# Matmuls of a pairwise interaction in 32x64 instead of 32x128 tiles, two field groups in each diagonal slot, and a reordered start

## What is computed

```python
e = jnp.stack([tbl_0[ids[:, 0]], ..., tbl_39[ids[:, 39]]], axis=1)      # 2048 x 40 x 32
iidx, jidx = jnp.triu_indices(40, k=1)
z = jnp.einsum('bpd,pde,bpe->bp', e[:, iidx, :], bilinear_matrices, e[:, jidx, :])
h = jnp.concatenate([z, dense_ctx], axis=1)                              # 2048 x 796
h = jnp.maximum(h @ W_top1 + b_top1, 0.0)                                # 512
h = jnp.maximum(h @ W_top2 + b_top2, 0.0)                                # 256
y = h @ W_top3
```

## Time and profile before

| what | value |
|---|---|
| median of 3 runs | 701.48 us (701.09 to 701.56) |
| profiled execution, own time | 700.91 us |
| its span in the profile | 699.1 us |
| PE busy | 662.1 us, 95% |
| DVE busy | 550.6 us, 79% |
| POOL busy | 463.0 us, 66% |
| ACT busy | 140.3 us, 20% |

### The profile page before, as it was taken

How to read it: one execution, slowest core, us unless ns; L and a number is a source line. 1 busy time by engine, 2 the same in 40 slices (tenths; PEclk the granted TensorE clock), 3 DMA queues, 4 the chain that set the end, 5 groups by cost and what they waited for, 6 DMA issues and landing times.

```text
span 699.1 us, 25209 instructions
## 1 busy us (share of the span) xinstructions
PE 662.1 (95%) x11496; PEld 413.8 (59%) x11496; DVE 550.6 (79%) x630; ACT 140.3 (20%) x350; POOL 463.0 (66%) x494
## 2 busy tenths in 40 slices
PE   1769989999999999999999999999999999999998
PEld 0645655566666666656655656565665656565656
DVE  5788889887898787878888787888878787678860
ACT  5411202112221202220220112211131112310002
POOL 6777777777777777777777777777777777700000
PEclk9999999999999999999999999999999999999999
DMA  6480102111120100200112000210101100000000
GB/s 201 133 294 16 16 15 51 25 16 15 16 61 16 16 15 16 61 15 16 16 20 57 16 15 16 61 16 15 16 16 16 16 15 16 16 4 2 3 1 1
DMA packets 23500, 23.89 MB, mean 34 GB/s; under 512 B 10917, under 2 KB 20705, under 8 KB 23265
## 3 DMA queue, kind: packets, MB, share of 16 engines
q0 software_dynamic: 15360, 7.90, 7.3%
q1 hardware_dynamic: 7418, 13.80, 5.9%
q10 hardware_dynamic: 616, 0.58, 0.3%
HBM read 22.18 MB, written 0.06 MB: 32 GB/s over the span
## 4 chain that ended last, share of the span: by engine, by line
PE 88%; DVE 6%; ACT 2%; issue 2%; DMA 1%; SPq 0%; ACTq 0%; DVEq 0%
PE Y L531 26%; PE ZL L558 24%; PE ZL L583 16%; PE H L509 8%; PE Y L539 6%; PE H L495 5%; DVE prod L760 4%; DVE one L746 2%; ACT xcols L668 1%; PE Y L592 1%; PE Y L601 1%; DVE prod L766 1%; DMA idx<-ids 1%; PE H L592 0%; DMA tab<-tbl 0%
## 5 line engine op out<-in xcount | busy, mean ns | idle before, releaser
L469 POOL DMA_INDIRECT rows<-tbl,idx x480 | 461.5, 962 | 148.1 <-issue 145.4
L760 DVE TENSOR_TENSOR prod<-Y,xcols 128x1024 f32<-128x1024 f32 x296 | 348.6, 1218 | 72.7 <-PE Y L531 72.4
L531 PE MATMUL Y<-xcols,mats 32*128 32x256 f32 x2880 | 207.7, 401 | 12.1 <-DVE prod L760 5.1
L558 PE MATMUL ZL<-prod,sel 128*32 128x256 f32 x3200 | 217.5, 383 | 0.9 <-ACT z L675 0.2
L531 PEld LDWEIGHTS Y<-xcols,mats 32*128 32x128 f32 x2880 | 132.5, 184 | 91.9 <-issue 74.2
L766 DVE TENSOR_TENSOR prod<-Y,xcols 128x1024 f32<-128x1024 f32 x104 | 122.8, 1219 | 46.0 <-PE Y L531 29.7
L668 ACT ACTIVATE xcols<-H 32x256 f32<-32x256 f32 (+3 forms) x223 | 83.8, 376 | 322.1 <-PE H L495 213.2
L558 PEld LDWEIGHTS ZL<-prod,sel 128*32 128x32 f32 x3200 | 93.2, 110 | 70.2 <-issue 26.8
L583 PE MATMUL ZL<-z,w_sb 128*32 128x256 f32 x1568 | 105.9, 379 | 0.0
L746 DVE TENSOR_SCALAR one<-idb,count 125x1024 bf16<-125x1024 f16 (+1 forms) x200 | 83.0, 450 | 0.0
L583 PEld LDWEIGHTS ZL<-z,w_sb 128*32 128x32 f32 x1568 | 51.7, 110 | 33.3
(11 more groups left out here) (30 smaller groups left out, 74.0 us busy)
## 6 DMA issues: line engine op xcount, KB each, us to landing
rows<-tbl,idx POOLq DMA_INDIRECT x480, 2.4
idb<-ids_turned SPq DMA_DIRECT2D x8, 768.0 KB
w_sb<-w SPq DMA_DIRECT2D x1, 1792.0 KB
mats<-m_wide SPq DMA_DIRECT2D x1, 1152.0 KB, 8.8
mats<-m_wide SPq DMA_DIRECT2D x1, 960.0 KB, 10.7
tab<-tbl SPq DMA_DIRECT2D x8, 112.0 KB
mats<-m_wide SPq DMA_DIRECT2D x1, 768.0 KB, 4.8
w_sb<-w SPq DMA_DIRECT2D x1, 512.0 KB
```

The costliest lines, as they stand in the source:

```text
L469: pool.indirect_dma_start(out=rows[:, slot, t, D * q:D * (q + 1)], out_offset=None, in_=tables[f], in_offset=bass.IndirectOffsetOnAxis(ap= ...
L531: last = pe.matmul(Y[:, bank, cols], mats[D * r:D * (r + 1), unit_cols(u)], xcols[D * r:D * (r + 1), n % 2, a, :], start=True, stop=True, ...
L558: last = pe.matmul(Z[D * q:D * (q + 1), :], sel[:, GF * (SPAN - 1 - o):GF * (SPAN - 1 - o) + 32], prod[:, (2 * s + q // 2) % PROD, q % 2, ...
L760: dve.tensor_tensor(prod[:, half, :, :].rearrange("p b (u c) -> p (b u) c", c=BLK), Y[:, pair:pair + 2, :].rearrange("p b (u c) -> p (b u) ...
```

## The change

Every unit, on the diagonal too, is computed in tiles of 32 x 64, so that eight matmuls stand side by side: 16 for each step. A diagonal slot holds the upper half of the pairs of one group and the lower half of another, in the four row strips of one slot. The products of such a slot need an `xcols` tile that is half of one group and half of the other; ACT makes it with two copies (`mix`) and DVE waits for it (`s_mix`). In step 24 each half of the products becomes two instructions of half the size. The order of the groups and the fields of the hot waves change. Ahead of step 0 each of the first five items writes a bank of its own (`stage`), one hot wave fewer is looked up there, and the row numbers of all blocks are turned at once. DVE copies most of them (`save_ids`), and SP issues their DMA and the first matrices ahead of the tables of the third wave. `hot_steps()` places one-hot tiles by a running count of DVE work against PE work, and their ring has 16 places instead of 12. The core of the diff:

```diff
-HOT = [(20, 21, 18, 23), (16, 13, 26, 11), (36, 33, 30, 15)]
+HOT = [(20, 21, 18, 23), (16, 25, 30, 15), (36, 33, 38, 11)]
-ORDER = [5, 4, 3, 2, 6, 7, 8, 9, 0, 1]
+ORDER = [5, 4, 7, 6, 3, 2, 8, 9, 0, 1]
...
-    def diagonal(G):
-        i = GF * G
-        units.append((G, G, [[(2, 3, i)], [(0, 1, i + 1), (3, 4, i + 1)],
-                             [(1, 2, i + 2)], [(0, 1, i + 3), (2, 3, i + 3)]]))
+    def upper(G):
+        units.append((G, G, [[(r + 1, GF, GF * G + r)] if r < GF - 1 else [] for r in range(GF)]))
+        return len(units) - 1
+    def lower(G):
+        units.append((G, G, [[(0, r, GF * G + r)] if r > 0 else [] for r in range(GF)]))
         return len(units) - 1
...
-            slots.append((diagonal(G[k]), diagonal(G[k + half])))
+            slots.append((upper(G[k]), lower(G[k + half])))
...
+def bank_of(k, r):
+    return (0, 1, 3, 2)[r] if any(on_diagonal(j) for j in slots(k // PAIR)) else r
+MIXED = {k: NG + m for m, k in enumerate(k for k in range(len(SLOTS)) if on_diagonal(k))}
...
-HOT_RING = 12
+HOT_RING = 16
-HEAD = [("turn", 0, 0), ("turn", 0, 1), ("hot", 0, 0), ("hot", 0, 1), ("turn", 0, 2), ("hot", 0, 2)]
-LANDED, PER_STEP = 14, 2.4
+HEAD = [("turn", 0, 0), ("turn", 0, 1), ("hot", 0, 0), ("turn", 0, 2), ("hot", 0, 1)]
+LANDED, PER_STEP = 12, 2.0
...
+    for s in range(NB * NS):
+        behind = max(behind, 0) + PRODUCTS - tensor_work(s)
+        while v < len(used) and (v < HOT_RING or used[v - HOT_RING] <= s):
+            if behind + ONE_HOT > LATE and used[v] > s + 1:
+                break
+            behind += ONE_HOT
+            at[v] = s
+            v += 1
...
+        def stage(at):
+            return Y[:, 5 - at, 0:BLK] if at < len(HEAD) else H[:, 0:BLK]
...
             spread_ids(0)
-            load_tables(sp, 2)
+            sp.wait_ge(s_rest_ids, 1)
+            sp.dma_start(ids_turned[1:NB].rearrange("n j c -> j n c"),
+                         idt[:, BLK:BATCH].rearrange("j (n c) -> j n c", c=BLK)).then_inc(s_idd, DMA)
             load_mats(0)
             load_mats(1)
-            sp.wait_ge(s_ids, 2)
-            sp.dma_start(ids_turned[1:NB].rearrange("n j c -> j n c"),
-                         idt[:, BLK:BATCH].rearrange("j (n c) -> j n c", c=BLK)).then_inc(s_idd, DMA)
+            load_tables(sp, 2)
             load_mats(2)
...
-                    if len(SLOTS[k]) == 1:
-                        u = SLOTS[k][0]
-                        a = UNITS[u][1]
+                    for c in range(2):
                         for r in range(GF):
-                            bank = 2 * ((2 * s + r // 2) % 3) + r % 2
-                            last = pe.matmul(Y[:, bank, cols], mats[D * r:D * (r + 1), unit_cols(u)],
-                                             xcols[D * r:D * (r + 1), n % 2, a, :], start=True, stop=True,
+                            u = SLOTS[k][1 if on_diagonal(k) and r > 2 * c else 0]
+                            b = bank_of(k, r)
+                            bank = 2 * ((2 * s + b // 2) % 3) + b % 2
+                            last = pe.matmul(Y[2 * D * c:2 * D * (c + 1), bank, cols],
+                                             mats[D * r:D * (r + 1), u * P + 2 * D * c:u * P + 2 * D * (c + 1)],
+                                             xcols[D * r:D * (r + 1), n % 2, UNITS[u][1], :], start=True, stop=True,
                                              skip_group_check=True)
-                    else:
-                        for h, u in enumerate(SLOTS[k]):
-                            G = UNITS[u][0]
-                            for r in range(2):
-                                bank = 2 * ((2 * s + h) % 3) + r
-                                last = pe.matmul(Y[:, bank, cols], mats[2 * D * r:2 * D * (r + 1), unit_cols(u)],
-                                                 xcols[2 * D * r:2 * D * (r + 1), n % 2, G, :], start=True, stop=True,
-                                                 skip_group_check=True)
...
+            def mix(n, k):
+                A, B = [UNITS[u][0] for u in SLOTS[k]]
+                act.wait_ge(s_free, mix_after(n, k) + 1)
+                act.activation(xcols[0:2 * D, n % 2, MIXED[k], :], xcols[0:2 * D, n % 2, B, :], ACT.Copy)
+                act.activation(xcols[2 * D:P, n % 2, MIXED[k], :], xcols[2 * D:P, n % 2, A, :], ACT.Copy).then_inc(s_mix, 1)
...
+            def save_ids():
+                dve.wait_ge(s_idt, 2)
+                for m in range(BT, MT, GF):
+                    bank, width = 1 + (m - BT) // GF, (min(m + GF, MT) - m) * P
+                    last = dve.tensor_copy(idt[:, m * P:m * P + width], Y[0:len(HOT_FIELDS), bank, 0:width])
+                last.then_inc(s_rest_ids, 1)
...
+                if h == 0 and on_diagonal(k1):
+                    dve.wait_ge(s_mix, max(mixes.index((n, k)) for k in (k0, k1) if on_diagonal(k)) + 1)
...
+                elif on_diagonal(k1):
+                    G, g, m = UNITS[SLOTS[k0][0]][0], UNITS[SLOTS[k1][h]][0], MIXED[k1]
+                    dve.tensor_tensor(prod[:, half, :, 0:BLK], Y[:, pair:pair + 2, 0:BLK],
+                                      xcols[:, n % 2, G:G + 1, :].to_broadcast([P, 2, BLK]), ALU.mult)
+                    dve.tensor_tensor(prod[:, half, :, BLK:BANK], Y[:, pair:pair + 2, BLK:BANK],
+                                      xcols[:, n % 2, g:m + 1:m - g, :], ALU.mult).then_inc(s_prod, 1)
```

More of the change, by code:

```diff
@@ L44 @@
 TAB_ROWS = [(0, 112), (112, HP)]
-PER = {f: 10 if f in (26, 11) else 8 for f in HOT_FIELDS}
+PER = {f: 10 if f in (38, 11) else 8 for f in HOT_FIELDS}
 PLACES = [max(PER[f] for f in wave) for wave in HOT]
@@ L170, in items @@
     turns = [(n, j) for n in range(NB) for j in range(len(cold(n))) if ("turn", n, j) not in HEAD]
-    hots = [(n, i) for n in range(1, NB) for i in hot(n)]
+    hots = [(n, i) for n in range(NB) for i in hot(n) if ("hot", n, i) not in HEAD]
     total = sum(BT * len(wave) for wave in COLD_FIRST[:sum(h[0] == "turn" for h in HEAD)])
@@ L184, in items @@
             half = None
-            continue
-        forced = False
+        elif hots and due[("hot", *hots[0])][0] == s + 1:
+            half = hots.pop(0)
+            at[s].append(("hot", *half, 0))
+        forced = bool(at[s])
         while turns and due[("turn", *turns[0])][0] <= s:
@@ L249, in hot_place, with tensor_work @@
                 if 0 <= v - hot_slot(n, i, 0) < PLACES[i])
+UNITS_SUMS, LAYER, MODE, TURNED, PLACE = 197, 43, 11, 46, 33
+PRODUCTS, ONE_HOT, LATE = 238, 44, 20
+def tensor_work(s):
+    n, w = divmod(s, NS)
+    work = UNITS_SUMS + MODE
+    if n > 0:
+        work += LAYER * len(mlp_part(w - 1 if w > 0 else NS - 1)[1])
+    for what, *which in ITEMS[s]:
+        work += TURNED if what == "turn" else PLACE * len(places(which[1], which[2]))
+    return work
 def hot_steps():
@@ L260, in hot_steps @@
                     used[hot_slot(n, i, t)] = s
-    at, pos = [0] * len(used), float(NB * NS)
-    for v in reversed(range(len(used))):
-        pos = min(used[v] - 2, pos - 0.9)
-        at[v] = -1 if used[v] < 0 else max(0, int(pos))
-    for v in range(HOT_RING, len(used)):
-        if at[v] >= 0:
-            at[v] = max(at[v], used[v - HOT_RING] + 1, at[v - 1])
-        assert used[v] < 0 or at[v] < used[v]
+    at, v, behind = [-1] * len(used), 0, 0
+    while v < len(used) and used[v] < 0:
+        v += 1
[6 more added lines that the diff above has]
+            at[v] = s
+            v += 1
+    assert all(u < 0 or a < u for a, u in zip(at, used))
     return at
@@ L645, in _ @@
         def _(act):
-            def save_ids(m0, m1, bank):
-                for m in range(m0, m1, GF):
-                    b, width = bank + (m - m0) // GF, (min(m + GF, m1) - m) * P
-                    last = act.activation(idt[:, m * P:m * P + width], Y[0:len(HOT_FIELDS), b, 0:width], ACT.Copy)
-                last.then_inc(s_ids, 1)
             def cast(i, part):
```

128 lines of the change are left out of this document (71 added, 57 removed).

## The result

| | before | after |
|---|---|---|
| median | 701.52 us (701.09 to 702.34) | 692.88 us (691.84 to 693.66) |
| span of the profiled execution | 699.1 us | 691.2 us |
| start of step 0 | 35.80 us | 37.13 us |
| start of block 1 | 115.80 us | 121.24 us |
| block 1 to the end of the span | 583.3 us | 570.0 us |

The ratio is 0.9875 (0.9857 to 0.9892). The kernel is faster by 8.6 us. I had forecast 21.6: the time lies within the range, but only two fifths of the gain came (8.6 / 21.6).

A forecast was written before the change was run, and what follows sets the result against it. PE was taken to bound blocks 1 to 7, with DVE close behind and ending most waits in block 0. Terms -2.8 + 3.9 - 23.7 + 0.3 - 1.7 + 2.4 = -21.6 us gave 680 us, range 668 to 694.

The forecast's parts named there:

- Diagonal slots: In each block, units of two steps fall from 1.93 to 1.03 us and one from 1.71 to 1.03: 2.5 us.
- Small tiles: Units group of 22 other steps a block falls from 1.07 to 1.03 us: 0.9 us a block.
- the loop through DVE: Units wait for half the previous step's products, then DVE waits for units; allows no step under about 2.55 us.
- Rival 2: Units stay at 1.07 us (8 us lost), late one-hot tiles or slow PE cost 4 in block 0: 692, chance 0.18.
- The `mix` copies cost nothing: Ten added ACT copies a block, some 0.40 us each, on a mostly idle ACT; DVE's wait for `s_mix` costs nothing.
- Step 24, -0.68 us: The step with a single diagonal slot in each block: its units fall from 1.71 to 1.03 us.
- The double turn: Last step of block 6 turned two waves, the second waiting 1.65 us for the bank; new order turns one: -1.7 us.
- One-hot lumps: Blocks 1 and 2: third hot wave's one-hot tiles, made in the steps using them, delay PE's places: +2.4 us for both.
- The head: Ahead of step 0: rows land at 25.1, then turning, look-up and copies; step 0 starts at 33.0 instead of 35.80: -2.8 us.
- Block 0: First block, held by DVE: more one-hot, table and split-product work, less waiting for diagonal units; +3.9 us on 80.0.
- The issue pace: Rival 4, units group: weight load and matmul pairs come at 29.2 ns, units take 1.21 us: 716, chance 0.06.
- turns in a row strip: Rival 5, units group: column halves of a row strip alternate, four more rounds of 0.216 us a step: 853, chance 0.02.

The follow-up runs named there:

- cheap diagonals alone: Kernel before with diagonal slots computed like the others, half of the diagonal pairs left out: 1209.6 us beside 1222.4 us for the kernel before, ratio 0.9892.
- the quiet head: Kernel after, with SP's third piece of matrices and everything queued behind it held until three waves are turned: 694.22 us, ratio 0.9905 to the kernel before.

## Why the prediction was right or wrong

**Diagonal slots, 2.5 us a block: right.** Steps 3 and 15 of block 4 fell from 3.80 to 2.91 and from 4.23 to 3.35, 0.89 and 0.88 for 0.90 forecast; cheap diagonals alone give 2.33 us.

**Small tiles, 0.04 us on each of 22 steps: the step that failed most.** Two things failed. The first is a size: from 1.07 us, 0.05 to 0.07 for the shorter first round and 0.03 for the late eighth start give 1.03 to 1.05, and I took the favourable end. Both parts came as said (0.05 and 0.03), and the group takes 1.05. The second is the sentence that the loop through DVE "has the units' duration in it, one to one", by which I multiplied the gain by all steps. DVE starts 0.04 us later behind the last unit's start than before, so steps that this loop binds got 0.01 to 0.02 longer. Measured 0.16 us a block instead of 0.9: 7 x 0.74 = 5.2 us. Together with the diagonals' 2.33 for 2.5 (7 x 0.15 = 1.0) the term of -23.7 (7 x 3.4 is 23.8, a slip without weight) should have been -17.5. Rival 2 (692) had the time, by another sum: the units are worth 6.2 us less and the rest came from the head and the seams, so that it fits is luck.

**"The `mix` copies cost nothing": wrong.** I priced them against ACT's idle time and DVE's wait for `s_mix`, both rightly, and did not ask what is queued behind them on ACT. There the copies of `Z` and of a hidden layer stand, and PE's sums wait for those: 6 x 0.49 = 2.9 us, taken back by the run that moved them.

**Step 24, -0.68 us: -0.28 measured.** It was PE work that went; the path through the seam is turn, copies, next units. The new order made three copies four. 0.37 us in seven blocks, six of them behind the start of block 1: 2.2 us; the run with three copies took all of it back.

**The double turn, -1.7: right**, by the earlier trace rows and the change of block 6, 82.00 to 78.55, which is 1.72 more than that of block 5, 79.99 to 78.26. But a turned wave more now stands in step 4, where there was none in the last block: +0.33 there.

**One-hot lumps, +2.4 in blocks 1 and 2: too much.** Against the 1.73 us of block 5 (and block 1's first step, which had no seam to lose), the two blocks came out some 1.4 us worse, and block 3 another 0.5 us better.

From block 1 on that makes 5.2 + 1.0 + 2.9 + 2.2 + 0.3 - 1.0 - 0.5 = 10.1 us of the 9.4 missed; the last 0.7 isn't traced to anything.

**The head, -2.8: +1.3 measured.** The step that failed is "I take twice the median, 25.1" for the landing of the third wave's rows. I had seen that the burst would meet the gathers and priced it as a slower transfer, 4.8 us from the issue's start at 20.06 (which is 24.9, not 25.1). Two things came in its place. The 12th gather was issued only at 23.29, since the change puts DVE's first one-hot tiles into one run without a pause and POOL's issue went on only behind it. And from there it took 6.9 us until the rows had landed, of which the quiet head gives back 3.8 behind the issue. I had priced POOL at its usual pace, although show an issue of 2.19 us: it starts at 42.55 and ends 0.11 us behind the run of 16 one-hot tiles of the earlier trace rows. My upper bound, rows at 27, was too low. No run changes DVE's tiles alone, so this half is read from the traces and not tested. Clock and look-up behind the wait were priced well: 5.25 us after a wait of 3.11 in the quiet head.

**Block 0, +3.9: right as a sum** (+4.1), so the head's delay went straight through to block 1. Of its parts, DVE's waits at the diagonal steps are gone as said (steps 3 and 15 fell by 0.91 and 0.81); the others weren't measured one by one.

**The issue pace and turns in a row strip: both fell.** Eight starts within 0.05 us are far from 29.2 ns a pair, which would need 0.20, and four rounds of eight tiles keep the time of four rounds of four. The Trainium skill (TensorE: Matmul & The Clock Gate, part 3, "The mechanism") lets a weight load overlap with a running matmul only when their row groups differ, though it also names a background weight buffer as a way to pull a load ahead. The windows above don't agree with the first: the two column halves of a row strip have one row group, yet from 661.43 to 661.60 weight loads run beside the first eight matmuls the whole time, and the group takes 1.05 us.

## What to carry to other kernels

Price both ends of a pipelined group: its start to the next group on its own engine, and its last start to the engine that waits for it. Ahead of calling added instructions free because their engine idles, list what stands behind them in that engine's order and who waits for that; here 0.83 us of cheap copies in a wrong place cost 0.49 us in each of six blocks. A burst of transfers delayed the rows of gathers at both places where it was put (3.8 and 3.1 us), so look for a place where no one waits for rows. And when the work of DVE is gathered into one run, look at what POOL has to issue beside it.
